# Cross-attention projections: two halves in one score bank, carried by six steps of a batch instead of twelve

## The reference

```python
q = jnp.einsum('oc,bct->bot', Wq, target) + bq[None, :, None]
k = jnp.einsum('oc,bcs->bos', Wk, source) + bk[None, :, None]
v = jnp.einsum('oc,bcs->bos', Wv, source) + bv[None, :, None]
# 16 heads of 16 channels
dot = jnp.einsum('bhdt,bhds->bhts', q, k) / math.sqrt(HEAD_DIM)
mask = target_mask[:, :, :, None] * source_mask[:, :, None, :]
dot = mask * dot - (1.0 - mask) * NEG
amap = jax.nn.softmax(dot, axis=-1) * mask
out = jnp.einsum('bhts,bhds->bhdt', amap, v)
```

## Time and profile before

| | |
|---|---|
| runs | 1543.59, 1549.84, 1550.4 us, median 1549.84 |
| profiled execution, span | 1545.7 us, clock granted to TensorE 0.963 on average |
| around the span | not given apart; the median of the runs is 4.1 us above the span |
| busy | PE 1438.5 us (93%), DVE 953.9, ACT 730.2, POOL 866.9 |
| cross-attention loop | from 310.27 to about 755 us; a batch takes 53 to 56 us, the last 64 us |

### The profile page before, as it was taken

How to read it: one execution, slowest core, us unless ns; L and a number is a source line. 1 busy time by engine, 2 the same in 40 slices (tenths; PEclk the granted TensorE clock), 3 DMA queues, 4 the chain that set the end, 5 groups by cost and what they waited for, 6 DMA issues and landing times. The chain is left out here.

```text
span 1545.7 us, 27131 instructions
## 1 busy us (share of the span) xinstructions
PE 1438.5 (93%) x7546; PEld 1024.1 (66%) x7546; DVE 953.9 (62%) x1426; ACT 730.2 (47%) x1416; POOL 866.9 (56%) x706
## 2 busy tenths in 40 slices
PE   6999999799999999998959999999999999999990
PEld 5878888434444444443547888888888888888870
DVE  2334343877888778888855555555555555555554
ACT  4212221178787787775433444434344443444233
POOL 4435332555677658644556646656666676476222
PEclk9999999989999999997869999999999999999995
DMA  5201003555485585651175546656666566473336
GB/s 202 85 22 51 14 32 66 84 97 70 88 148 117 89 147 115 92 109 47 56 242 140 152 99 168 169 115 174 153 161 159 156 165 164 118 196 81 64 58 231
DMA packets 93630, 181.36 MB, mean 117 GB/s; under 512 B 19097, under 2 KB 21913, under 8 KB 92473
## 3 DMA queue, kind: packets, MB, share of 16 engines
q1 hardware_dynamic: 73800, 133.04, 34.1%
q0 software_dynamic: 18544, 46.13, 14.9%
q10 hardware_dynamic: 1152, 0.52, 0.2%
HBM read 116.32 MB, written 33.73 MB: 97 GB/s over the span
## 5 line engine op out<-in xcount | busy, mean ns | idle before, releaser
L952 DVE TENSOR_REDUCE stage<-ps_a 128x2 f32<-128x1024 f32 x256 | 300.2, 1218 | 74.5 <-PE ps_a L1301 73.8
L750 ACT ACTIVATE probs<-ps_b 128x512 f32<-128x512 f32 x504 | 274.2, 596 | 52.2 <-PE ps_b L1316 47.7
L2086 POOL TENSOR_TENSOR we_split<-we_raw,we_split 128x512 f32 (+1 forms) x192 | 248.6, 1532 | 84.0 <-ACT we_split L2077 82.1
L2408 PE MATMUL ps_y<-we_split,hT 128*128 x912 | 231.5, 402 | 2.9 <-DVE hT L2330 2.9
L2408 PE MATMUL ps_u<-we_split,xT 128*128 x912 | 230.9, 402 | 0.0
L2408 PE MATMUL ps_g<-we_split,xT 128*128 x912 | 227.0, 397 | 0.5 <-POOL we_split L2086 0.5
L2408 PEld LDWEIGHTS ps_g<-we_split,xT 128*128 128x128 f32 x912 | 172.0, 189 | 42.9 <-issue 0.9
L2408 PEld LDWEIGHTS ps_y<-we_split,hT 128*128 128x128 f32 x912 | 165.5, 188 | 38.1 <-issue 3.3
L2408 PEld LDWEIGHTS ps_u<-we_split,xT 128*128 128x128 f32 x912 | 166.2, 189 | 34.1
L2250 ACT ACTIVATE hT<-ps_h 128x512 fp32r<-128x512 f32 x76 | 45.2, 595 | 303.2 <-PE ps_h L2380 263.4
L2198 POOL DMA_INDIRECT scratch_acc<-x_keep,to_rows x76 | 121.2, 1594 | 109.3 <-issue 49.9
(11 more groups left out here) (345 smaller groups left out, 2208.9 us busy)
## 6 DMA issues: line engine op xcount, KB each, us to landing
we_raw<-in_w_expert SPq DMA_DIRECT2D x180, 256.0 KB
stack<-xT_raw SPq DMA_DIRECT2D x192, 128.0 KB, 5.5
we_bias<-in_b_expert SPq DMA_DIRECT2D x16, 768.0 KB, 4.4
stage<-in_w SPq DMA_DIRECT2D x5, 1024.0 KB, 5.4
xT_raw<-in_xT SPq DMA_DIRECT2D x4, 1024.0 KB, 6.8
x_tok<-in_x POOLq DMA_DIRECT2D x16, 256.0 KB, 3.0
acc_sb<-scratch_acc SPq DMA_DIRECT2D x8, 512.0 KB, 8.0
out<-res_sb SPq DMA_DIRECT2D x8, 512.0 KB, 4.6
```

Source lines behind the costliest of these rows:

```text
L750: nc.scalar.activation(probs[:, n % 3, h], src[:], ACT.Exp, scale=DH ** -0.5).then_inc(b_kept, 1)
L952: nc.vector.tensor_reduce(out[:, :, i, k % NC], ps_a[i][:], AX.X, ALU.max, negate=True).then_inc(a_kept[i], 1)
L2086: nc.gpsimd.tensor_tensor(lo, W["raw"][:, k, c], hi, ALU.subtract).then_inc(W["lo"], 1)
L2408: mm = nc.tensor.matmul(out[:], left[:, a, c], w[:, bass.ds(par, 1), k, b, c].squeeze(1), start=(n == 0), stop=(n == len(passes) - 1))
```

## The change

Both halves of a q or k projection go into one bank of 512 columns, as matmuls of 512 columns; two pieces of v go into the two halves of one bank, still as matmuls of 256 columns. One ACTIVATE of 128x512 empties each. They stand behind s = 2, 4, 6, 10, 12 and 14; s = 3, 5, 7, 11, 13 and 15 carry nothing. This holds for the projections made inside the loop (`is_whole` for q and k; all of v from batch 1); those made ahead of the loop stay as they were.

```diff
-            if s in (2, 3, 4, 5) and b + 1 < B:
-                return [("qk", b + 1, 2 + (s - 2) // 2, s % 2)]
-            if s in (6, 7, 10, 11) and b + 1 < B:
-                return [("v", b + 1, (6, 7, 10, 11).index(s))]
+            if s in (2, 4) and b + 1 < B:
+                return [("qk", b + 1, 2 + (s - 2) // 2)]
+            if s in (6, 10) and b + 1 < B:
+                return [("v", b + 1, (6, 10).index(s))]
...
-            if s >= 12 and b + 2 < B:
-                return [("qk", b + 2, (s - 12) // 2, s % 2)]
+            if s in (12, 14) and b + 2 < B:
+                return [("qk", b + 2, (s - 12) // 2)]
             return []
+
+        def is_whole(b, i):
+            return b >= 2 or (b == 1 and i >= 2)
...
-                nc.scalar.activation(full[:, k % 2, h * C:(h + 1) * C], src[:, 0:C], ACT.Identity,
+                cols = slice(0, 2 * C) if is_whole(b, i) else slice(h * C, (h + 1) * C)
+                nc.scalar.activation(full[:, k % 2, cols], src[:, 0:cols.stop - cols.start], ACT.Identity,
                                      bias=bias_qk[:, i % 2, i // 2:i // 2 + 1]).then_inc(b_kept, 1)
...
-                nc.scalar.activation(v_stage[:, c // 2, c % 2], src[:, 0:C], ACT.Copy).then_inc(b_kept, 1)
+                if b >= 1:
+                    nc.scalar.activation(v_stage[:, c // 2], src[:].rearrange("p (a c) -> p a c", a=2),
+                                         ACT.Copy).then_inc(b_kept, 1)
+                else:
+                    nc.scalar.activation(v_stage[:, c // 2, c % 2], src[:, 0:C], ACT.Copy).then_inc(b_kept, 1)
...
-                        mm = nc.tensor.matmul(out[:, 0:C], w_qk_cut[wi][:, qk, c, o], rhs, start=(n == 0), stop=(n == 5))
+                        mm = nc.tensor.matmul(out[:, 0:n_cols], w_qk_cut[wi][:, qk, c, o], rhs, start=(n == 0),
+                                              stop=(n == 5))
...
+                for at, sc in enumerate(pieces):
+                    part = out[:, at * C:(at + 1) * C]
...
-                    project_qk(b + 1, 2 + (s - 2) // 2, s % 2)
-                if s in (6, 7, 10, 11) and b + 1 < B:
-                    project_v(b + 1, (6, 7, 10, 11).index(s))
+                if s in (2, 4) and b + 1 < B:
+                    project_qk(b + 1, 2 + (s - 2) // 2, 1)
+                if s in (6, 10) and b + 1 < B:
+                    project_v(b + 1, *((0, 1) if s == 6 else (2, 3)))
```

More of the change, by code:

```diff
@@ L282, in uses_of_ring @@
             order += [("rank", 3), ("turn", NT - 2), ("turn", NT - 1), ("logits", B - 1)]
-            return {use: i for i, use in enumerate(order)}, early
-        USE, EARLY = uses_of_ring()
+            at = {}
+            for i, use in enumerate(order):
+                if use[0] == "qk" and len(use) == 3:
+                    at.update({use + (h,): i for h in range(2)})
+                elif use[0] == "v" and use[1] >= 1:
+                    at.update({("v", use[1], 2 * use[2] + j): i for j in range(2)})
+                else:
+                    at[use] = i
+            return at, early, len(order)
+        USE, EARLY, USES = uses_of_ring()
         cuts = [("w_qk",), ("x", 2), ("ctx", 2, 0), ("ctx", 2, 1), ("w_v",)]
@@ L1254, in project_qk @@
                     pe.wait_ge(y_stats, 3 * (2 * b + 2))
-                if b >= 2 and o == 0 and not qk and h == 0:
+                if b >= 2 and o == 0 and not qk:
                     pe.wait_ge(cut_step, CUT["x", b])
@@ L1259, in project_qk @@
                 out = bank("qk", b, i, h)
-                cols = slice(h * C, (h + 1) * C)
+                cols = slice(0, 2 * C) if is_whole(b, i) else slice(h * C, (h + 1) * C)
+                n_cols = cols.stop - cols.start
                 if b < 2:
@@ L1263, in project_qk @@
                         rhs = ctx_in[b % 2][:, c, cols] if qk else x[:, 2 * b + c, cols]
-                        mm = nc.tensor.matmul(out[:, 0:C], w_qk[:, qk, c, o], rhs, start=(c == 0), stop=(c == 1))
+                        mm = nc.tensor.matmul(out[:, 0:n_cols], w_qk[:, qk, c, o], rhs, start=(c == 0), stop=(c == 1))
                 else:
@@ L1268, in project_qk, with project_v @@
                         rhs = (ctx_cut if qk else x_cut)[xi][:, c, cols]
[L1269 removed]
+                        mm = nc.tensor.matmul(out[:, 0:n_cols], w_qk_cut[wi][:, qk, c, o], rhs, start=(n == 0),
+                                              stop=(n == 5))
                 mm.then_inc(b_made, 1)
[L1272 to L1273 removed]
+            def project_v(b, *pieces):
+                if b == 2 and pieces[0] == 0:
                     pe.wait_ge(cut_step, CUT["w_v",])
[L1275 to L1285 removed]
+                out = bank("v", b, pieces[0])
+                for at, sc in enumerate(pieces):
+                    part = out[:, at * C:(at + 1) * C]
+                    rows = slice(sc * P, (sc + 1) * P)
+                    if b < 2:
+                        for c in range(2):
+                            mm = nc.tensor.matmul(part, ctx_in[b % 2][:, c, rows], w2[:, 2, c, :],
+                                                  start=(c == 0), stop=(c == 1))
+                    else:
+                        passes = [(c, wi, xi) for wi, xi in SPLITS for c in range(2)]
+                        for n, (c, wi, xi) in enumerate(passes):
+                            mm = nc.tensor.matmul(part, ctx_cut[xi][:, c, rows], w_v[:, wi, c], start=(n == 0),
+                                                  stop=(n == 5))
                 mm.then_inc(b_made, 1)
```

33 lines of the change are left out of this document (10 added, 23 removed).

## The result

| | before | changed |
|---|---|---|
| median of 7 runs each | 1549.84 us | 1558.69 us |
| lowest and highest | 1543.59, 1552.42 | 1550.92, 1560.76 |
| profiled execution, span | 1545.7 us | 1556.4 us |
| granted clock, mean | 0.963 | 0.962 |

The ratio is 1.0054, 95% interval [1.0036, 1.0071]: the changed kernel is 8.4 us slower, between 5.6 and 11. The forecast was 1560.5 with a range of 1551 to 1568.

What follows compares the result with a forecast made beforehand. PE was taken to bound projection steps, a PE-ACT chain the empty ones. Terms: v 2.1, q/k before maxima 5.5, q/k otherwise 1.9, s = 7 to 9 1.5; +11.0 us on 1549.84 gives 1560.8, stated 1560.5, range 1551 to 1568.

Steps and rivals of the forecast that it cites:

- The heavy step: Step carrying a whole projection or two v pieces: 3.92 us, where a step with one piece took 3.22.
- late exponential: Behind a wide q or k evacuation, e0's exponential starts at e0 + 0.76, 0.17 to 0.2 us later than before.
- rival C: Wide matmuls cost PE no more than 256-column ones, 0.115 us a pass: -7 us, 1542.5; chance 0.04.
- The empty step: Step carrying no projection: about 2.69 us, with 0.37 us of PE newly idle; a pair costs +0.15 us.
- rival B: PE runs through an empty step at its own 2.32 us, pairs shorten by 0.2: -8 us, 1542; chance 0.08.
- q, k before maxima: Pairs at s = 4, 5 and 12, 13: +0.42 us each, 13 pairs, 5.5 us.
- Rival A: Only PE's bubbles cost; ACT absorbs the later exponential and DVE keeps up: +4 to +7 us, 1555.5; chance 0.25.
- q, k otherwise: Six pairs at s = 14 and three at s = 2: 0.15 + 0.06 us each, 1.9 us.
- s = 2 and 3: Four batches where DVE takes moments and rules the pair: costed at 0, possibly down to -0.5 us each.
- s = 7 to 9: PE comes 0.5 us earlier to DVE's reduction behind a short s = 7: 6 x 0.25 = 1.5 us.
- What comes earlier: Earlier q, k, v for POOL's splits, earlier ctx cut, ACT relieved by about 1 us a batch: costed at nothing.
- rival D: TensorE's clock falls more often behind router logits: +10 us more in all five places, 1566 in two or three; chance 0.16.

Runs made afterwards that it cites:

- e0: Not a run: a step's first score matmuls on PE, whose exponential ACT makes; e0 + 0.76 means 0.76 us after they start.
- halving the emptied bank: The changed kernel with ACT emptying only 256 of the 512 columns of a whole q or k; 1553.74 us in one execution.
- odd-step kernel: The changed kernel with its six heavy steps moved to s = 3, 5, 7, 11, 13, 15; 1562.08 us, 1.0077 of the kernel before.
- only v: The changed kernel with q and k back in halves, each behind its own step; 1554.98 us, 1.0036 of the kernel before.
- two kernels without a low part: Kernel before and changed kernel, each without DVE's subtraction for the row maxima's low part; 1546.95 and 1553.18 us, 0.9992 and 1.0034 of the kernel before.
- only q, k: The changed kernel with v back in single pieces at s = 6, 7, 10, 11; 1557.46 us, 1.0053 of the kernel before.
- the two groups: Profiled executions with q and k at s = 12 to 15 whole, or in single pieces; mean low-clock time 10.2 against 3.4 us.

## Why the prediction was right, point by point

- **The heavy step.** 3.92 us forecast; 3.92 to 3.97 behind v from the third batch on, 4.12 to 4.16 behind q and k at s = 4 and 12, which is 3.92 and the late exponential, and 4.00 to 4.03 at s = 14. The wide pass costs 0.23 us: rival C is out. The 131 ns that the Trainium skill gives for such a matmul ("TensorE: Matmul & The Clock Gate", section "Back-to-back issue gap") do not hold for this one.
- **The empty step.** 2.69 forecast; 2.54 to 2.60 measured, since the exponential with which such a window begins is itself late; the pair is what counts. Of the 14 pairs with v, 13 cost +0.06 to +0.17, 0.15 forecast; the other, at s = 6, 7 of the second batch, is 0.67 shorter. The pair at s = 14, 15 is 4.03 + 2.54 = 6.57 where it was 3.22 + 3.24 = 6.46, so rival B, which needed a shorter pair, is out.
- **The late exponential.** e0 + 0.76 forecast, e0 + 0.76 in the trace. q, k before maxima: +0.42 forecast, +0.42 to +0.49 in 12 of 13 pairs (+0.13 in the other, s = 4, 5 of the fourth batch, where s = 4 took 3.53 us before and not 3.23); halving the emptied bank took 0.14 to 0.19 off. Rival A is out as the whole story.
- **q, k otherwise.** 0.21 forecast for each, +0.08 to +0.12 at s = 14, 15: mis-sized. The delay of 0.06 did not add up. The three at s = 2, 3 scatter: +0.36 and +0.09 in the second and fifth batch, +0.76 in the first with the low clock.
- **s = 2 and 3.** The step that failed is "rearranging PE costs nothing in such a batch", costed at 0 with a bound of -0.5 each. The traces show -0.76, -0.57, -1.44 and -0.45 in the third, fourth, sixth and seventh batch, 3.2 us together. PE's wait for DVE is filled with the second half of the projection; in the odd-step kernel, where that half stands behind the wait, the gain is gone. The row for it was at hand: PE was busy 3.76 of 4.83 us at s = 3 of the sixth batch, 1.07 us idle. How much is gained in one batch scatters, since the pair is not steady there: in the sixth batch the kernel before took 0.29 us less in its second profiled execution, and only v, with q and k in single pieces, took 0.88 less. The two kernels without a low part give 0.98, 0.35, 0.55 and 0.54 in the third to the sixth batch.
- **s = 7 to 9.** +1.5 forecast and +1.57 measured. That PE comes 0.5 us earlier behind a short s = 7 was right: the table above gives 0.55. The prediction took DVE's subtraction as 1.20 us; that was already the form beside POOL's operation, it is 0.18 by itself, and the cast ahead of it stretches too. How long the two take in a batch changes from one execution to the next, so that the sum of the six batches came out at 1.5 is in part luck. Without the subtraction the change costs 0.6 us here; with q and k alone, where s = 7 is as long as before, 2.3. The two causes overlap: at s = 8, 9 only v from the second batch on and only q, k together cost 1.3 + 2.3 us, the change 1.6.
- **What comes earlier** was costed at nothing. Where POOL stands when DVE casts and subtracts may be part of it, and that had a price. At s = 6, 7 of the second batch it went the other way, -0.67, in a place where PE waited 0.70 us for the DMA of the maxima before.
- **The clock (rival D).** 0 in the forecast; about 2 us by the means of the two groups, suggestive only. In the two profiles that are subtracted here it is +2.0 us in the batches 1 to 7, and the last batch, with less low clock than before, is 2.8 us shorter.
- **The median.** The forecast put the sum of 11.0 us on the median of three. The steps at full clock make +6.4 us of the 8.4; the remaining 2 are of the size of the clock's share. Whether they are the clock's stays open.

The sum came out near for the main term, which was right, and because a gain that I missed (-3.2) and falls that I did not count (+2) partly cancelled. That the median came within 2 us of the forecast is in this part luck.

## What to carry to other kernels

Cut windows at single steps and ask for each kind of step what limits it; if one kind has no idle time on the busiest engine and the other has, packing the work of two steps of the first kind into one makes a step of the second kind, and its idle time is lost each time. Half as many instructions of twice the width saved ACT 11 us of busy time here, and the program was 8 us slower; 2.1 us of that is the wide one standing in front of the instruction on which a chain without slack begins. Work moved ahead of a wait is gained, but look at once for what the earlier engine meets next: here DVE operations held beside POOL's, DVE's reductions for the maxima, and a DMA just in time.
